# Expert outputs in a mixture-of-experts layer: gathered and summed in a last stage, or weighted on chip and scatter-added to the output in memory

## What is computed

```python
def _L1_ffn_ref(x, Wg, bg, bias, W1, b1, W2, b2):
    logits = jnp.einsum('sbd,de->sbe', x, Wg) + bg + bias
    vals, idx = jax.lax.top_k(logits, TOP_K)                 # TOP_K = 2 of 16
    w = jax.nn.softmax(vals - jnp.max(vals, axis=-1, keepdims=True), axis=-1)
    cw = jnp.einsum('sbk,sbke->sbe', w, jax.nn.one_hot(idx, NUM_EXPERTS, dtype=x.dtype))
    h = jax.nn.relu(jnp.einsum('sbd,edh->esbh', x, W1) + b1[:, None, None, :])   # 256 -> 512
    y = jnp.einsum('esbh,ehd->esbd', h, W2) + b2[:, None, None, :]               # 512 -> 256
    return jnp.einsum('esbd,sbe->sbd', y, cw)
...
x = x + _L1_attn_ref(_layernorm(x, axis=-1), ...)
x = x + _L1_ffn_ref(_layernorm(x, axis=-1), ...)
return x
```

## Time and profile before

| | us |
|---|---|
| median of 2 runs | 1748.57 (1747.04 to 1750.1) |
| span of the profiled execution | 1744.6 |
| router, with its normalisation | about 1307 to 1395 |
| expert loop | about 1396 to 1701 |
| last stage, from its first load to the end | 1705.8 to 1744.6 |

### The profile page before, as it was taken

How to read it: one execution, slowest core, us unless ns; L and a number is a source line. 1 busy time by engine, 2 the same in 40 slices (tenths; PEclk the granted TensorE clock), 3 DMA queues, 4 the chain that set the end, 5 groups by cost and what they waited for, 6 DMA issues and landing times. The chain is left out here.

```text
span 1744.6 us, 40230 instructions
## 1 busy us (share of the span) xinstructions
PE 1527.0 (88%) x14142; PEld 1006.2 (58%) x14144; DVE 1184.2 (68%) x2319; ACT 979.9 (56%) x2029; POOL 419.2 (24%) x617
## 2 busy tenths in 40 slices
PE   5979999999999999998789975999794489999990
PEld 4843333333333333334678874888683189999980
DVE  6768999999999999941478848654558922222225
ACT  2425888888888888882154521444232055555543
POOL 3148001010110101000103325422212045555540
PEclk9966999999999999997899985999897589999995
DMA  5942223223233323010100001233208632222218
GB/s 180 292 157 38 45 45 58 45 57 61 49 69 53 61 52 64 9 21 20 14 0 1 1 14 50 78 102 94 76 0 288 196 114 71 69 72 70 69 61 289
DMA packets 122967, 135.24 MB, mean 78 GB/s; under 512 B 29301, under 2 KB 93833, under 8 KB 122697
## 3 DMA queue, kind: packets, MB, share of 16 engines
q1 hardware_dynamic: 110056, 107.60, 24.3%
q0 software_dynamic: 7584, 20.72, 3.6%
q10 hardware_dynamic: 5184, 4.98, 0.8%
HBM read 92.23 MB, written 36.04 MB: 74 GB/s over the span
## 5 line engine op out<-in xcount | busy, mean ns | idle before, releaser
L1873 DVE TENSOR_REDUCE mx<-ps 128x1 f32<-128x1024 f32 x512 | 611.2, 1218 | 23.2 <-PE ps L2004 19.0
L1916 ACT ACTIVATE PR<-ps 128x512 f32<-128x512 f32 x1024 | 557.2, 599 | 100.5 <-PE ps L2049 46.9
L2004 PE MATMUL ps<-KQ 48*128 48x512 f32 x1024 | 391.5, 465 | 10.7 <-PEq L249 6.0
L2049 PE MATMUL ps<-KQ 50*128 50x512 f32 x1024 | 380.6, 451 | 0.0
L2033 PE MATMUL ps<-PR,VO 128*32 128x256 f32 x4096 | 330.6, 395 | 9.2 <-ACT PR L1916 8.7
L2049 PEld LDWEIGHTS ps<-KQ 50*128 50x128 f32 x1024 | 156.7, 187 | 217.2 <-ACT PR L1916 200.0
L2033 PEld LDWEIGHTS ps<-PR,VO 128*32 128x32 f32 x4096 | 81.1, 108 | 196.1 <-ACT PR L1916 98.0
L2004 PEld LDWEIGHTS ps<-KQ 48*128 48x128 f32 x1024 | 160.3, 194 | 30.3 <-DVE mx L1873 24.0
L1760 PEld LDWEIGHTS ps<-e_xinT,e_w 128*128 128x128 f32 x1264 | 155.0, 194 | 5.8 <-issue 1.8
L1760 PE MATMUL ps<-e_xinT,e_w 128*128 128x128 f32 x1264 | 155.7, 277 | 1.1 <-ACT e_xinT L1692 1.1
L1750 PE MATMUL ps<-eW,e_hiddenT 128*128 x632 | 149.3, 379 | 0.0
(11 more groups left out here) (273 smaller groups left out, 2069.6 us busy)
## 6 DMA issues: line engine op xcount, KB each, us to landing
qk_parts<-parts SPq DMA_DIRECT2D x8, 2048.0 KB, 7.9
TB<-toeplitz_lines SPq DMA_DIRECT2D x32, 512.0 KB, 6.5
KQ<-qk_parts SPq DMA_DIRECT2D x96, 128.0 KB, 4.8
KQ<-qk_parts SPq DMA_DIRECT2D x192, 64.0 KB, 2.4
eW<-in_L_ffn_W SPq DMA_DIRECT2D x16, 512.0 KB, 6.8
eW<-in_L_ffn_W SPq DMA_DIRECT2D x8, 1024.0 KB, 12.3
e_got<-expert_outputs SPq DMA_DIRECT2D x16, 512.0 KB, 9.5
X<-in_L_attn_x SPq DMA_DIRECT2D x8, 512.0 KB, 4.7
```

The source lines that it names most:

```text
L1873: nc.vector.tensor_reduce(mx[:, u % RING, h * QT + q:h * QT + q + 1], ps[:, b:b + 2].rearrange("p a n -> p (a n)"), AX, ALU.max, negate=Tr ...
L1916: nc.scalar.activation(PR[:, kt % 2, h], ps[:, st_bank(u, s)], ACT.Exp).then_inc(exp_done, 1)
L2004: made = nc.tensor.matmul(ps[:, max_bank(u, t) + k], of_tile(queries(u % RING), h, q), kq[half(h, KROWS), 0, h % HR, k * BANK:(k + 1) * BA ...
L2049: nc.tensor.matmul(ps[:, st_bank(u, s)], kq[half(h, AROWS), 0, h % HR, kt * P:(kt + 1) * P], queries(u % RING)[half(h, AROWS), qc, h % HR] ...
```

## The change

The experts' results go straight to the output. The store of `X` moves to the block that makes it: SP stores each chunk as soon as it is added, and one spare tile of 128 rows behind the output for the padding slots. In the router the one-hot products carry the token number plus one and the slot's weight instead of two parts of a row number, so all of them become float32, PLACES becomes 4 (the tiles are twice as large), and the three operations for the weights stand ahead of them. In the loop VectorE multiplies each tile of `y` by its slots' weights, in a second operation that waits for the first. The scatter becomes an indirect DMA with `compute_op=ALU.add`, which adds to the rows in memory, and two of them must never be under way together, since each token has two rows to be added at one place: POOL waits before each for the landing of the one before. The last stage is gone.

```diff
@@ def ssm_output
         with nc.Block() as block:
+            @block.sync
+            def _(sp):
+                for c in range(NC):
+                    sp.wait_ge(o_added, c + 3)
+                    sp.dma_start(out_tiles[:, CT * c:CT * (c + 1), :], X[:, CT * c:CT * (c + 1), :]).then_inc(x_stored, 16)
+                sp.dma_start(out_tiles[:, NT:NT + 1, :], X[:, 0:1, :]).then_inc(x_stored, 16)
+                sp.wait_ge(x_stored, 16 * (NC + 1))
@@ def moe, the router
-            PLACES = 8
+            PLACES = 4
...
-            lane = sbuf(s0, "r_lane", [P, P], BF16)
+            lane = sbuf(s0, "r_lane", [P, P])
...
-            in_lane = sbuf(s0, "r_in_lane", [P, 2, PLACES, P], BF16)
-            in_tile = sbuf(s0, "r_in_tile", [P, 2, PLACES, 2, MTP], BF16)
+            in_lane = sbuf(s0, "r_in_lane", [P, 2, PLACES, P])
+            in_tile = sbuf(s0, "r_in_tile", [P, 2, PLACES, 2, MTP])
...
-                    nc.gpsimd.iota(oi[:], pattern=[[P, MT]], base=0, channel_multiplier=1).then_inc(iotas, 1)
+                    nc.gpsimd.iota(oi[:], pattern=[[0, MT]], base=T + 1, channel_multiplier=1).then_inc(iotas, 1)
+                    nc.gpsimd.iota(ki[:], pattern=[[P, NT]], base=1, channel_multiplier=1).then_inc(iotas, 1)
...
-                    for dst, src in ((lane, ai), (tile_no, ti), (part_no, pi), (own, oi)):
+                    for dst, src in ((lane, ai), (tile_no, ti), (part_no, pi), (own, oi), (tok, ki)):
...
+                    dve.wait_ge(r_exp, 1)
+                    step(nc.vector.tensor_scalar(ex[:, 2], ex[:, 1], 1.0, None, ALU.add))
+                    step(nc.vector.reciprocal(weight[:, 0], ex[:, 2]))
+                    step(nc.vector.tensor_tensor(weight[:, 1], ex[:, 1], weight[:, 0], op=ALU.mult))
                     dve.wait_ge(c_done, 1)
...
-                            nc.vector.tensor_scalar(in_tile[:, s, j, 0], tile_no[:], tile, part_no[:], ALU.is_equal, ALU.mult).then_inc(one_hot, 1)
-                            nc.vector.tensor_scalar(in_tile[:, s, j, 1], tile_no[:], tile, float(FREE + NT * s + i + j), ALU.is_equal, ALU.mult).then_inc(one_hot, 1)
+                            nc.vector.tensor_scalar(in_tile[:, s, j, 0], tile_no[:], tile, tok[:, t:t + 1], ALU.is_equal, ALU.mult).then_inc(one_hot, 1)
+                            nc.vector.tensor_scalar(in_tile[:, s, j, 1], tile_no[:], tile, weight[:, s, t:t + 1], ALU.is_equal, ALU.mult).then_inc(one_hot, 1)
...
-                    dve.wait_ge(r_exp, 1)
-                    step(nc.vector.tensor_scalar(ex[:, 2], ex[:, 1], 1.0, None, ALU.add))
-                    step(nc.vector.reciprocal(weight[:, 0], ex[:, 2]))
-                    step(nc.vector.tensor_tensor(weight[:, 1], ex[:, 1], weight[:, 0], op=ALU.mult))
...
-                    step(nc.vector.scalar_tensor_tensor(tab[:], ps[:, 0, MTP:MTP + MT], float(P), tab[:], op0=ALU.mult, op1=ALU.add))
+                    steps.mark(nc.vector.tensor_copy(slot_weight[:], ps[:, 0, MTP:MTP + MT]))
...
-                    step(nc.vector.tensor_copy(y_row[:], tab[:]))
+                    step(nc.vector.tensor_scalar(out_row[:], tab[:], -1.0, None, ALU.add))
@@ def moe, the expert loop
                         pool.wait_ge(y_kept, k + 3)
-                        nc.gpsimd.indirect_dma_start(y_rows, bass.IndirectOffsetOnAxis(ap=y_row[:, k:k + 1].bitcast(U32), axis=0), y[:, z], None).then_inc(stored[z], 16)
+                        if k > 0:
+                            pool.wait_ge(stored[1 - z], 16 * ((k - 1) // 2 + 1))
+                        nc.gpsimd.indirect_dma_start(out, bass.IndirectOffsetOnAxis(ap=out_row[:, k:k + 1].bitcast(U32), axis=0), y[:, z], None,
+                                                     compute_op=ALU.add).then_inc(stored[z], 16)
...
-                        nc.vector.tensor_tensor(y[:, z], ps[:, Y_BANK[z], 0:D], b2b[:, ds(e, 1), :].rearrange("p a d -> p (a d)"), op=ALU.add).then_inc(y_kept, 1)
+                        nc.vector.tensor_tensor(y[:, z], ps[:, Y_BANK[z], 0:D], b2b[:, ds(e, 1), :].rearrange("p a d -> p (a d)"), op=ALU.add).then_inc(y_biased, 1)
+                        dve.wait_ge(y_biased, k + 1)
+                        nc.vector.tensor_scalar(y[:, z], y[:, z], slot_weight[:, ds(k, 1)], None, ALU.mult).then_inc(y_kept, 1)
@@ the last stage
-        with ExitStack() as s2:
...
-                            rows = y_rows[FREE * P + s * T + CW * c:FREE * P + s * T + CW * (c + 1), :]
-                            sp.dma_start(got[:, r, s], rows.rearrange("(k p) d -> p k d", p=P)).then_inc(loaded[r][s], 16)
...
-                        act.dma_start(out_tiles[:, CT * c:CT * (c + 1), :], X[:, CT * c:CT * (c + 1), :]).then_inc(out_stored, 16)
...
-                            last = nc.scalar.activation(second[:, c % 2, k], got[:, r, 1, k], ACT.Copy, scale=weight[:, 1, CT * c + k:CT * c + k + 1])
...
-                            nc.vector.scalar_tensor_tensor(X[:, t], got[:, r, 0, k], weight[:, 0, t:t + 1], X[:, t], op0=ALU.mult, op1=ALU.add).then_inc(first_added, 1)
...
-                        nc.vector.tensor_tensor(chunk, chunk, flat(second[:, c % 2]), op=ALU.add).then_inc(added, 1)
```

More of the change, by code:

```diff
@@ L139, in transformer_kernel @@
     x_rows = x_in.rearrange("b s d -> (b s) d")
-    out_rows = out.rearrange("b s d -> (b s) d")
     x_tiles = x_rows.rearrange("(t p) d -> p t d", p=P)
-    out_tiles = out_rows.rearrange("(t p) d -> p t d", p=P)
+    out_tiles = out.rearrange("(t p) d -> p t d", p=P)
     by_k = lambda w: w.rearrange("(k p) n -> p k n", p=P)
@@ L433, in transformer_kernel @@
             feed_forward(nc, sem, sbuf, ps, X, ident, ffw, ssi)
-        ssm(nc, sem, sbuf, ps, X, ident, ssi, bm_in, cm_in, dm_in, lnw_in, lnb_in, wout_in, bout_in, by_k)
+        ssm(nc, sem, sbuf, ps, X, ident, ssi, out_tiles, bm_in, cm_in, dm_in, lnw_in, lnb_in, wout_in, bout_in, by_k)
         early.close()
         reuse_sems()
-        moe(nc, sem, sbuf, ps, X, ident, out_tiles, wg_in, bg_in, bias_in, w1_in, b1_in, w2_in, b2_in)
+        moe(nc, sem, sbuf, ps, X, ident, out, wg_in, bg_in, bias_in, w1_in, b1_in, w2_in, b2_in)
 FH = 1024
@@ L1255, in _ @@
                     batches(pe, body, written_out=True)
-        ssm_output(nc, sem, sbuf, ps, X, Y, ident, woT, lnwb, turned)
+        ssm_output(nc, sem, sbuf, ps, X, Y, ident, out_tiles, woT, lnwb, turned)
 def toeplitz(line):
@@ L1264, in toeplitz, with ssm_output @@
     return bass.AP(tensor=a.tensor, offset=a.offset, ap=[[1, P], *a.ap])
-def ssm_output(nc, sem, sbuf, ps, X, Y, ident, woT, lnwb, turned):
+def ssm_output(nc, sem, sbuf, ps, X, Y, ident, out_tiles, woT, lnwb, turned):
     with ExitStack() as st:
@@ L1272, in ssm_output @@
         norm = ChunkNorm(nc, sem, sbuf, st, "lny", Y)
-        n_tr, g_ready, o_done, o_added = (sem("so_" + n) for n in ("n_tr", "g_ready", "done", "added"))
+        n_tr, g_ready, o_done, o_added, x_stored = (sem("so_" + n) for n in ("n_tr", "g_ready", "done", "added", "x_stored"))
         with nc.Block() as block:
+            @block.sync
[5 more added lines that the diff above has]
+                sp.wait_ge(x_stored, 16 * (NC + 1))
             @block.gpsimd
@@ L1340, in _, with moe @@
                 chunks(pe, body)
-def moe(nc, sem, sbuf, ps, X, ident, out_tiles, wg_in, bg_in, bias_in, w1_in, b1_in, w2_in, b2_in):
-    FREE = -(-MT // NT) * NT
+def moe(nc, sem, sbuf, ps, X, ident, out, wg_in, bg_in, bias_in, w1_in, b1_in, w2_in, b2_in):
     xrows = nc.dram_tensor("expert_inputs", [T, D], F32, kind="Internal").ap()
-    y_rows = nc.dram_tensor("expert_outputs", [FREE * P + 2 * T, D], F32, kind="Internal").ap()
     with ExitStack() as st:
@@ L1354, in moe @@
         b1T = sbuf(st, "b1T", [P, E * EK])
-        weight = sbuf(st, "weight", [P, 2, NT])
+        slot_weight = sbuf(st, "slot_weight", [P, MT])
         owner = sbuf(st, "owner", [P, MT], I32)
         token = sbuf(st, "token", [P, MT], I32)
-        y_row = sbuf(st, "y_row", [P, MT], I32)
+        out_row = sbuf(st, "out_row", [P, MT], I32)
         w_loaded = [sem(f"e_w_loaded{q}") for q in range(2)]
@@ L1374, in moe @@
             ex = sbuf(s0, "r_exp", [P, 3, NT])
-            PLACES = 8
+            PLACES = 4
             ai, pi = (sbuf(s0, "r_" + n, [P, w], I32) for n, w in (("ai", P), ("pi", 1)))
             oi, own = sbuf(s0, "r_oi", [P, MT], I32), sbuf(s0, "r_own", [P, MT])
-            lane = sbuf(s0, "r_lane", [P, P], BF16)
+            ki, tok = sbuf(s0, "r_ki", [P, NT], I32), sbuf(s0, "r_tok", [P, NT])
+            weight = sbuf(s0, "r_weight", [P, 2, NT])
+            lane = sbuf(s0, "r_lane", [P, P])
             MTP = MT + MT % 2
-            tile_no = sbuf(s0, "r_tile_no", [P, MTP], BF16)
+            tile_no = sbuf(s0, "r_tile_no", [P, MTP])
             part_no = sbuf(s0, "r_part_no", [P, 1])
@@ L1384, in moe @@
             at2 = sbuf(s0, "r_at2", [P, 2, 2, NT])
-            in_lane = sbuf(s0, "r_in_lane", [P, 2, PLACES, P], BF16)
```

(15 more changed lines are left out.)

46 lines of the change are left out of this document (4 added, 42 removed).

## The result

| | us |
|---|---|
| kernel before, median of 2 | 1748.57 (1747.04 to 1750.1) |
| changed kernel, median of 2 | 1794.36 (1790.38 to 1798.33) |
| ratio | 1.027 (95% interval 1.023 to 1.030) |
| span of the profiled execution, before and after | 1744.6 and 1788.7 |
| predicted | 1727, range 1713 to 1824 |

The change costs 46 us. The prediction said 22 less, and gave the case that came true, "the scatter sets the pace", 0.22. The measured time lies inside its range, but on the other side of the old time.

A forecast was written before the change was run, and what follows sets the result against it. The prediction took TensorE to bound the loop at 3.69 us a tile and the last stage to be memory traffic. 1744.6 - 36.0 + 4.3 + 10.0 = 1722.9, with the median's 4.0 1727 us; range 1713 to 1824.

The forecast's parts named there:

- the scatter sets the pace: Rival at POOL's wait before each scatter: landing 4.65, cycle 4.93 us, time 1824; chance 0.22.
- change 2: Loop, one scatter at a time: landing 3.15 plus restart 0.28, cycle 3.43 rounded to 3.45, hidden under TensorE's 3.69 us.
- POOL's work: Scatter in the loop: an add costs POOL nothing more or up to +0.99 us; 0.1 taken, by the gathers.
- Data: Scatter in the loop: destination rows must be read as well, +0.6 us, taken in full.
- The rule of half the rate: Scatter's DMA traffic: two source reads halve the rate, so 0.5 us becomes 1.0, landing 2.95, cycle 3.2.
- Row by row: Rival in the scatter's landing: each DMA engine adds its 8 rows one by one, cycle 13 us, time near 2450; chance 0.07.
- Restart: POOL's start behind a semaphore in the loop: 0.28 us from a landing to the next scatter.
- The size of the reserve: Loop: the scatter's cycle fits into TensorE's 3.69 us a tile with 0.24 us to spare.
- The last stage: Kernel's end: removing this stage saves 36.0 us; some 8 us remain after the last scatter, 4.3 of them drain.
- Storing `X`: Before the router: the block waits for the last chunk's store and the spare tile, +4.3 us (3.6 to 6.4).
- The one-hots: Router: float32 one-hots take VectorE 0.53 + 0.15 = 0.68 us a place, +9.7 us for 64 places.
- The second operation on `y`: VectorE in the loop: 0.41 us more a tile, hidden in a 1.20 us idle gap; 32 us at most otherwise.

The follow-up runs named there:

- swapped run: Changed kernel with POOL's two waits before a scatter in the other order, first the previous scatter's landing, then `y`: 1754.8 us, ratio 1.004.
- runs with half the bytes: Changed kernel adding only 128 of each row's 256 values: 1761.8 us; or only 64 of each tile's 128 rows: 1745.3 us.
- run with plain writes: Changed kernel with plain scatters instead of adds, still one at a time, the sum in memory left out: 1726.1 us, ratio 0.986.
- its repeat: The changed kernel itself, unaltered, once more on the same chip as the run with the waits swapped: 1798.7 us, ratio 1.026.

## Why the prediction was wrong

**The step that failed** is change 2, the size of the scatter's cycle: 3.43 forecast (rounded to 3.45), 4.63 measured. The rest of that step was right: that landing and restart add up to the period, that it decides from 3.97, and 78 x (c - 3.69) as the price. Put c = 4.63 into it and it gives 1727 + 73 = 1800, for 1794 measured. The cycle was too short in three of its terms. The first two alone (c = 4.08) take the forecast gain away; the third turns it into a loss.

| term | predicted | measured | error |
|---|---|---|---|
| POOL's work on an add | 1.09 (0.99 + 0.1) | 1.58 | 0.49 |
| from its end to the landing | 2.06 (1.46 + 0.6) | 2.22 | 0.16 |
| restart of POOL behind a landing | 0.28 | 0.83 | 0.55 |

1. *POOL's work.* Bounds of nothing and 0.99 more; I took 0.1, by the gathers, which take no longer than plain scatters. The measured 0.59 more lies near the middle. The gather was no guide to it: it reads from memory, but it adds nothing. Why an add takes POOL longer, no run shows. An operation of which no row shows anything should stand in the middle of its bounds.
2. *Data.* +0.6 forecast, +0.76 measured. The traffic of one add goes from 1604.0 to 1605.3, 1.3 us (windows of 0.25 us), where a plain scatter took 0.5:

```profile
1604.00:1604.25 0.25, 0.25 (x3) 0.23 (x2) 0.00 (x0) 0.23 (x1) 0.25 (x1) 1.00 1.40 66
1604.25:1604.50 0.25, 0.25 (x3) 0.20 (x3) 0.00 (x0) 0.25 (x2) 0.25 (x1) 1.00 0.86 98
1604.50:1604.75 0.25, 0.25 (x3) 0.22 (x2) 0.00 (x0) 0.15 (x1) 0.25 (x1) 1.00 0.87 135
1604.75:1605.00 0.25, 0.25 (x3) 0.22 (x2) 0.00 (x0) 0.11 (x1) 0.02 (x1) 1.00 0.95 148
1605.00:1605.25 0.25, 0.25 (x3) 0.22 (x2) 0.00 (x0) 0.25 (x1) 0.00 (x0) 1.00 0.49 74
```

The rule of half the rate for two reads (the Trainium skill, Collectives: The Full Stack, "The bandwidth ceiling") gave 1.0, by the prediction's estimate; here it is somewhat more. "Row by row" is out: it wanted a cycle of 13 us. This agrees with what the prediction drew from the Trainium skill (DMA: Bandwidth & Descriptors, "Two DMAs through the same engine are not ordered"), that additions overlap instead of going row by row; no run here tests additions to one row.

3. *Restart.* This is the largest term, and I did not see that it was open. The 0.28 was read from a row in which the scatter waits for `y` alone; I then used it for a scatter with two waits, of which the other comes last. The swapped run has 3.8 + 0.28 = 4.08 and so shows that 0.28 was right for the wait written first and wrong for the place where the change had put the landing's. The runs with half the bytes bear the other value out: 4.12 - 3.3 = 0.82 and 3.96 - 3.1 = 0.86. With the waits in this order the prediction's formula gives 1727 + 78 x 0.39 = 1757, for 1754.8 measured: within 1% of the kernel before.

**The size of the reserve** made this decisive. I gave 0.24 us to spare a chance of 0.45. Three terms, each with an error of a few tenths possible and nearly all of it upward, deserve less than that.

**What was right.** The last stage is gone: the last scatter starts 6.9 us before the end, where 45.9 lay before (1698.65 to 1744.6), and 7.8 were forecast. That is two misses against each other: it lands after 3.8 and not 3.15, and the drain is 2.68 and not 4.31. The last two scatters start 4.36 us apart (1777.45 and 1781.81), where I had put 3.45. Storing `X`: from the last addition's end, 1302.2, to the router at 1306.9 are 4.7 us, before 1.3: +3.5, forecast 4.3. The one-hots: 0.66 a place, forecast 0.68; VectorE never waited in them (0.0 in the rows above), so TensorE did not bound them. Its granted clock over 1350 to 1400 rose from 0.50, its lower level of 1.2 GHz, to 0.87 (0.50 up to 1362, 1.00 from 1364), and it was busy for 35.7 instead of 22.5 of 50 us. The second operation on `y`: 0.40, hidden. The run with plain writes gives the four together: 1726 for 1727. That it fits to 1 us is partly luck: the terms above miss by 0.8 to 1.3 us each, its cycle is 3.72 and not 3.69, and one execution differs from another by more than that (in the changed kernel, its repeat and the swapped run the first scatter starts at 1420.8, 1427.6 and 1424.8).

## What to carry to other kernels

When a transfer has to be awaited before the next may start, its period is POOL's work, plus the flight, plus the restart behind the semaphore, and all three must fit under the work that hides them; take each from a row of the same kind of wait, or from the middle of its bounds. Where a POOL transfer has two waits of which the landing of a DMA is met last, write that one first, and look at the separate wait in the trace: here the order alone was 44 us. And before serialising, ask which pairs can meet at all: the data's structure (one expert, no token twice) made nearly all the waits needless.

## What the runs showed of the hardware

- A scatter-add of 128 rows of 1 KB keeps POOL busy for 1.58 us (plain: 0.99) and lands 3.8 us after its start (plain: 2.4). With 64 rows it is still 1.43 and 3.1, with 128 rows of 512 B 1.58 and 3.3.
- Adds to different rows overlap: one started every 3.69 us, at TensorE's pace, each landing after 3.8.
- POOL starts a scatter 0.28 us after the semaphore that it waits for last, VectorE's or a landing's, if that wait is the only one or the one written first, and 0.76 to 0.86 us after it if it is the one written second (seen for a landing only).
- The drain of POOL's sequencer at the end of the loop's block took 4.31 us behind plain scatters and 2.68 behind adds of 128 rows, but 3.66 behind adds of 64 rows and 4.11 behind adds in the run where POOL issued no gathers. What sets it stays open.
